# Linear attention with a following FFN on one core: k by token from the DMA queue's transpose instead of TensorE's

## The chip, the cores and the metric

One core of one Trainium2 chip runs the whole program. The metric is the device time of one execution in microseconds (us), lower is better; a kernel's time is the median of its runs.

## The reference

x has 8 batches of 1024 tokens with 512 channels. One attention layer with pre-norm and one linear FFN follow each other, both with a residual:

```python
qkv = layernorm(x) @ W_attn + b_attn            # 512 -> 3 * 512
q, k = elu(q) + 1, elu(k) + 1                   # 16 heads of 32 channels
def step(carry, inp):                           # over the tokens, in order
    kv = kv + kt[..., :, None] * vt[..., None, :]
    ksum = ksum + kt
    return (kv, ksum), (qt @ kv) / (qt @ ksum + 1e-6)
x = x + y @ W_proj + b_proj
x = x + fp16(e4m3(layernorm(x))) @ fp16(e4m3(weight)).T + bias
```

## The kernel before

The 8192 tokens are cut into 64 token tiles of 128; n numbers them. Four tiles make a block j, and 8 tiles a batch, at whose start the carried state begins anew. The main loop goes over n = 0 to 65, written out for each engine in its own order: TensorE, ScalarE (act), VectorE (dve), GpSimd (pool) and SP (sp), whose queue issues every DMA. They are tied by semaphores; each engine takes its instructions in order, so what stands behind a waiting instruction waits too.

For one block the projection makes 12 results of 128x512: i = 0 to 3 are q and 4 to 7 are k, with channels on partitions and the block's 512 tokens in the columns, and 8 to 11 are v for its four tiles, with tokens on partitions. Each is 12 matmuls of fp16 (high and low part of the data and of the weight). They are made one block ahead, three in each tile's iteration (`ahead(chunks(n))`), two before and one behind the place of `k_tokens`; in n = 59 to 61 there is one each, in n = 62 and 63 none. `phi` on ScalarE (exp and relu) and VectorE (min and add) turns q and k into features in `qk`, fp32.

For tile n TensorE goes through `scores(n)` (k against q, in halves of 64 tokens, into S), `from_state(n)` (q against the carried state), two feature results, the transposes of `k_tokens(n + 1)`, the third result, `values(n)` (masked scores times v), `update(n + 1)` (called delta here: k by token times v, which gives what the next tile adds to the state), `proj(n - 1)` and `ffn(n - 2)`. `update` needs k with tokens on partitions, as the stationary operand. That is `k_tokens`: four transposes of 128x128 fp32 on TensorE against `ident` into one bank, then one copy by ScalarE into `ktok`, which has two buffers.

ScalarE's order in iteration n is: copy of half the scores (sm), x2 to fp8 and to bf16 for tile n - 2, exp and relu of the first result, the high part of the layer norm (xnhl), exp and relu of the second, the copy of ktok for tile n + 1, exp and relu of the third, the high part of y, and the copy of ffn's result (o). VectorE and GpSimd do the norms' statistics and scaling, the low parts, the masks, the state and the residual.

Other transposes already go by the queue: the layer norm's two fp16 parts (xnhl to xt, 8 blocks of 128x128), y's two parts (yhl to yt, 8 blocks) and x2 in bf16 (x2b to x2t, 4 blocks). SP's order in iteration n is y's transpose for tile n - 1, x2's for n - 2, xt's for n + 8, a load of x for n + 10, and the store of tile n - 2, which waits for VectorE's last addition. For the last four tiles TensorE transposes y itself.

The matmul results, the transposes, delta, proj and ffn take turns in a ring of four banks of PSUM (`take`): each waits until the one four places before it has been read. In the listing S is the other half of PSUM. `raw` is a buffer of 24 KB per partition for the weights as they are loaded; its third part (raw[:, 2]) is read last by the preparation of v's weight (`s_wl` at 6).

Of the kernel before, what the change touches and what calls it, by code (L numbers as in the profile page):

```python
# [10 lines left out]
BF16 = mybir.dt.bfloat16  # L11
F8 = mybir.dt.float8e4
I32 = mybir.dt.int32

D = 512
B = 8
T = 1024
P = 128
HALF = P // 2
W = 33  # L20
NT = B * T // P
# [67 lines left out]
def build(nc, x_d, wa_d, ba_d, wp_d, bp_d, wf_d, bf_d, out_d):  # L89
    ctx = ExitStack()  # L90
    with ctx:
# [6 lines left out]
        def sem(name):  # L98
            return ctx.enter_context(nc.semaphore(f"s_{name}"))
# [51 lines left out]
        w_f = raw[:, 0, :, :]  # L151
        w_8 = raw[:, 1, 0:2, :].rearrange("p a n -> p (a n)").bitcast(F8).rearrange("p (i k n) -> p i k n", i=2, k=4)
        w_lo, w_hi = w_8[:, 0, :, :], w_8[:, 1, :, :]
        w_b = raw[:, 1, 2:4, :].rearrange("p a n -> p (a n)").bitcast(BF16).rearrange("p (k n) -> p k n", k=4)


# [4 lines left out]
        s_wft = sem("wft")  # L161
        s_xt = [sem(f"xt{t}") for t in range(4)]
        s_yt = [sem(f"yt{i}") for i in range(2)]
        s_x2t = [sem(f"x2t{i}") for i in range(2)]

        s_t1, s_qkv, s_score, s_ktr, s_delta = sem("t1"), sem("qkv"), sem("score"), sem("ktr"), sem("delta")
        s_av, s_ty, s_proj, s_ffn, s_t2, s_most = sem("av"), sem("ty"), sem("proj"), sem("ffn"), sem("t2"), sem("most")

        s_xth, s_size, s_wh, s_relu, s_whi = sem("xth"), sem("size"), sem("wh"), sem("relu"), sem("whi")
        s_xhi, s_ktok, s_scopy, s_wph = sem("xhi"), sem("ktok"), sem("scopy"), sem("wph")  # L170
        s_x28, s_x2b, s_yh, s_yth, s_o16 = sem("x28"), sem("x2b"), sem("yh"), sem("yth"), sem("o16")

        s_bn1, s_var1, s_bn2, s_var2 = sem("bn1"), sem("var1"), sem("bn2"), sem("var2")
# [24 lines left out]
        def parts(n):  # L198
            j, c = divmod(n, 4)
            return qk[j % 2], v1[j % 2], j, c  # L200
# [15 lines left out]
        def _(e):  # L216
# [66 lines left out]
                    mm = matmul(out[:, :], a, b, m == 0, m == 11)  # L283
                mm.then_inc(s_qkv, 1)

            def k_tokens(n):
                src, v, j, c = parts(n)
                cols = slice(c * P, (c + 1) * P)
                out = take(("ktok", n), s_ktok, n + 1)
                for g in range(4):  # L290
                    pe.wait_ge(s_phi, phi_count(j, 4 + g))
                transposes(out, [src[:, 4 + g, cols] for g in range(4)]).then_inc(s_ktr, 1)

            def update(n):

# [106 lines left out]
            for i in range(12):  # L402
                proj_qkv(0, i)
                if i in (0, 2, 11):
                    most((0, 2, 11).index(i) + 1)
                if i == 9:
                    k_tokens(0)
            update(0)
            for n in range(NT + 2):
                j, c = divmod(n, 4)  # L410
                if n < NT:
                    scores(n)
                    from_state(n)
                    ahead(chunks(n)[0])
                    if tail(n - 1):
                        t_y(n - 1)
                    if n + 1 < NT:
                        k_tokens(n + 1)
                    if n:
                        ahead(chunks(n)[1])  # L420
                    values(n)
                    if n + 1 < NT:
                        update(n + 1)
                    if n == 0:
                        ahead(chunks(n)[1])
                if 1 <= n <= NT:
                    proj(n - 1)
                if n == NT - 1:
                    t_y(n)
                if n >= 2:  # L430
                    t2(n - 2)
                    ffn(n - 2)

        @block.scalar
        def _(e):
# [45 lines left out]
            def ln1_parts(m):  # L481
# [2 lines left out]
                    act.wait_ge(s_xt[m % 4], 16 * (m // 4 - 1))  # L484
                copy(xnhl[:, m % 4, 0, :], xn[:, m % 2, :]).then_inc(s_xhi, 1)

            def k_tokens(n):
                act.wait_ge(s_ktr, n + 1)
                if n >= 2:
                    act.wait_ge(s_delta, n - 1)  # L490
                copy(ktok[:, n % 2, :], bank["ktok", n][:, :]).then_inc(s_ktok, 1)

            def scores(n):
                if not alone(n):
# [72 lines left out]
            phi(0, 6)  # L567
            ln1_parts(7)
            phi(0, 7)
            proj_size()  # L570
            k_tokens(0)
            ffn_half()
            for n in range(NT + 2):
                j, c = divmod(n, 4)
                if n < NT:
                    scores(n)
                    if n == 0:
                        proj_weight()
                    if n >= 2:
                        t2(n - 2)  # L580
                    ahead(chunks(n)[0][:1])
                    if n + 8 < NT:
                        ln1_parts(n + 8)
                    ahead(chunks(n)[0][1:])
                    if tail(n - 1):
                        t_y(n - 1)
                    if n + 1 < NT:
                        k_tokens(n + 1)
                    if n:
                        ahead(chunks(n)[1])  # L590
                    values(n)
                    if n == 0:
                        ahead(chunks(n)[1])
                if n == NT - 1:
                    t_y(n)
                if n >= NT:
                    t2(n - 2)
                if n >= 2:
                    ffn(n - 2)

        @block.vector
        def _(e):
# [361 lines left out]
        def _(e):  # L964
# [17 lines left out]
            def t_y(n):  # L982
                if not tail(n):
                    sp.wait_ge(s_yl, n + 1)
                    if n >= 2:
                        sp.wait_ge(s_proj, n - 1)
                    e.dma_start(yt[:, n % 2, :, :], yhl[:, n % 2, :, :].rearrange("p a n -> p (a n)"),
                                transpose=True).then_inc(s_yt[n % 2], 16)

            def t2(n):  # L990
                if n < NT - 2:
                    sp.wait_ge(s_x2b, n + 1)
# [30 lines left out]
            for t in range(4):  # L1023
                t1(4 + t)
            for n in range(NT + 2):
                if 1 <= n <= NT:
                    t_y(n - 1)
                if n >= 2:
# [38 lines left out]
```

## Time and profile before

| | |
|---|---|
| time, median of 3 runs | 1013.76 us (1013.19 to 1015.6) |
| the profiled execution | 1014.31 us, span 1012.6 us |
| TensorE busy | 982.0 us (97%) |
| VectorE, GpSimd, ScalarE busy | 69%, 53%, 46% |
| mean granted TensorE clock | 0.991 |
| DMA, mean share of 16 engines | 34.9% (the queue), 81 GB/s |
| chain that ended last | TensorE 91%, VectorE 3%, GpSimd 2% |

PE is TensorE and PEld its weight loads, DVE VectorE, ACT ScalarE, POOL GpSimd, SP SyncE, and SPq the queue's issues. Busy times are of the profiled execution and overlap between engines. L231 is the line of every matmul, L235 that of every transpose on TensorE, L439 that of ScalarE's copies, whatever their place; so the tile's name tells them apart. The granted clock is given as a share of 2.4 GHz.

### The profile page before, as it was taken

The page shows a single profiled execution, that of the slowest core. Times are in us where ns is not written, and L with a number is a line of the kernel's source. Part 1 is how long each engine was busy: PE and PEld are TensorE (multiplying, and loading weights), DVE is VectorE, ACT ScalarE, POOL GpSimd, SP SyncE. Part 2 cuts the span into 40 slices and gives each one's busy share as a digit, 9 for nine tenths or more (in the row PEclk, how much of TensorE's full clock was granted, in tenths as well). Part 3 has the DMA queues.
Part 4 walks back from the last instruction along what each step waited for, and adds up shares of the span by engine and source line. Part 5 has one row for each costly group of instructions (what it writes and reads, how often), then busy time and mean ns, then how long its engine had stood idle before and what let it go on. Part 6 is the DMA issues. An engine that isn't in the chain of part 4 may idle for free.

```text
span 1012.6 us, 43583 instructions
## 1 busy us (share of the span) xinstructions
PE 982.0 (97%) x19504; PEld 549.5 (54%) x19504; DVE 701.7 (69%) x1448; ACT 463.6 (46%) x714; POOL 535.3 (53%) x523
## 2 busy tenths in 40 slices
PE   5999999999999999999999999999999999999895
PEld 2454555555555555555555555555555555555552
DVE  6888677677767677676767767767776767754573
ACT  5753452544545364453535445254454535445222
POOL 3545675564565565465456456456456556533323
PEclk9999999999999999999999999999999999999997
DMA  8714334333334334334342244343332543322211
GB/s 271 113 35 80 94 76 81 86 77 84 80 75 91 75 75 94 72 83 88 71 96 74 71 93 79 78 88 75 83 83 75 90 77 75 81 44 54 55 35 48
DMA packets 185355, 82.51 MB, mean 81 GB/s; under 512 B 165840, under 2 KB 165840, under 8 KB 185168
## 3 DMA queue, kind: packets, MB, share of 16 engines
q1 hardware_dynamic: 185168, 79.73, 34.9%
q8 instruction: 153, 2.51, 1.0%
q14 instruction: 34, 0.28, 0.1%
HBM read 22.81 MB, written 16.78 MB: 39 GB/s over the span
## 4 chain that ended last, share of the span: by engine, by line
PE 91%; DVE 3%; POOL 2%; ACT 1%; issue 1%; DMA 0%; ACTq 0%; POOLq 0%
PE R L231 74%; PE S L231 15%; PE R L235 3%; POOL st L875 1%; DVE st L606 1%; DVE xs L696 0%; POOL xn L877 0%; POOL x L877 0%; DVE raw L800 0%; DMA xs<-in_L_attn_x 0%; POOL xs L918 0%; POOL sm L902 0%; DVE qk L629 0%; DVE wpl L778 0%; ACT qk L448 0%
## 5 line engine op out<-in xcount | busy, mean ns | idle before, releaser
L231 PE MATMUL R<-xt,wh 128*128 128x512 f16 x1024 | 306.2, 381 | 2.4 <-ACT wh L439 2.4
L629 DVE SCALAR_TENSOR_TENSOR qk<-qk,rel 128x512 f32<-128x512 f32 x128 | 141.3, 1105 | 151.1 <-ACT rel L451 151.1
L909 POOL TENSOR_TENSOR yhl<-y,yhl 128x512 f16<-128x512 f32 x60 | 69.9, 1165 | 311.2 <-ACT yhl L439 311.2
L231 PE MATMUL R<-xt,wl 128*128 128x512 f16 x512 | 194.4, 381 | 0.0
L875 POOL TENSOR_TENSOR st<-st,half 128x1 f32<-128x1 f32 x128 | 94.8, 741 | 138.3 <-DVE st L611 125.4
L231 PE MATMUL R<-wh,xt 128*128 128x512 f16 x512 | 160.3, 379 | 0.0
L231 PEld LDWEIGHTS R<-xt,wh 128*128 128x128 f16 x1024 | 96.7, 98 | 108.4 <-DVE xt L744 2.6
L231 PE MATMUL R<-wph,yt 128*128 128x512 f16 x512 | 134.6, 386 | 2.8 <-DVE yt L689 2.8
L439 ACT ACTIVATE yhl<-y 128x512 f16<-128x512 f32 x60 | 37.8, 630 | 209.5 <-DVE y L683 209.5
L448 ACT ACTIVATE qk<-R,bqk,wm 128x512 f32<-128x512 f32 x128 | 98.9, 772 | 54.0 <-PE R L231 54.0
L897 POOL TENSOR_TENSOR xs<-xs,bp 128x512 f32<-128x512 f32 x64 | 110.4, 1731 | 0.1
L623 DVE TENSOR_TENSOR xnhl<-xn,xnhl 128x512 f16<-128x512 f32 x56 | 88.3, 1576 | 22.3 <-ACT xnhl L439 22.3
L451 ACT ACTIVATE rel<-R,bqk,wm 128x512 f32<-128x512 f32 x128 | 98.5, 769 | 1.7 <-DVE qk L629 1.7
L231 PE MATMUL R<-wl,xt 128*128 128x512 f16 x256 | 97.0, 379 | 0.0
L606 DVE BATCH_NORM_STATS2 st<-xs 128x6 f32<-128x512 f32 x128 | 88.4, 690 | 5.9 <-DMA xs<-in_L_attn_x 3.7
L918 POOL TENSOR_TENSOR xs<-xs,bf 128x512 f32<-128x512 f32 x64 | 81.7, 1277 | 5.3
L231 PEld LDWEIGHTS R<-xt,wl 128*128 128x128 f16 x512 | 50.3, 98 | 61.1 <-issue 1.1
L231 PEld LDWEIGHTS S<-v,sm 64*64 64x64 f32 x4096 | 65.9, 134 | 31.1 <-issue 29.1
L231 PEld LDWEIGHTS R<-wh,xt 128*128 128x128 f16 x512 | 50.1, 98 | 55.6
L439 ACT ACTIVATE o<-R 128x512 f16<-128x512 f32 x64 | 38.3, 598 | 91.3 <-PE R L231 91.3
L231 PE MATMUL S<-v,sm 64*64 64x33 f32 x4096 | 73.2, 221 | 5.0 <-POOL sm L902 3.2
L637 DVE SCALAR_TENSOR_TENSOR v<-R,wm,bv 128x512 f32<-128x512 f32 x64 | 47.8, 747 | 42.4 <-PE R L231 42.1
(91 smaller groups left out, 1498.0 us busy)
## 6 DMA issues: line engine op xcount, KB each, us to landing
xs<-in_L_attn_x SPq DMA_DIRECT2D x64, 256.0 KB, 3.8
out<-xs SPq DMA_DIRECT2D x64, 256.0 KB, 2.4
raw<-in_L_attn_W_attn SPq DMA_DIRECT2D x3, 1024.0 KB, 9.6
xs<-in_L_attn_W_proj SPq DMA_DIRECT2D x4, 256.0 KB
raw<-in_L_ffn_weight SPq DMA_DIRECT2D x1, 1024.0 KB, 16.2
x2t<-x2b SPq DMA_TRANSPOSE x62, 2.3
xt<-xnhl SPq DMA_TRANSPOSE x60, 3.1
yt<-yhl SPq DMA_TRANSPOSE x60, 3.2
```

The costliest lines, as they stand in the source:

```text
L231: return e.matmul(out, a, b, start=start, stop=stop, skip_group_check=True)
L439: return e.activation(out, in_, ACT.Copy, **more)
L448: e.activation(dst[:, i, :], bank["qkv", j, i][:, :], ACT.Exp, scale=UN[i // 4], bias=bqk[:, i:i + 1])
L451: e.activation(rel[:, u % 2, :], bank["qkv", j, i][:, :], ACT.Relu, scale=UN[i // 4], bias=bqk[:, i:i + 1]).then_inc(s_relu, 1)
L606: e.bn_stats(row[:, 0:6], src).then_inc(s_bn, 1)
L623: e.tensor_tensor(xnhl[:, m % 4, 1, :], xn[:, m % 2, :], xnhl[:, m % 4, 0, :], ALU.subtract).then_inc(s_xlo, 1)
L629: e.scalar_tensor_tensor(qk[j % 2][:, i, :], qk[j % 2][:, i, :], 1.0, rel[:, (u - 1) % 2, :], ALU.min, ALU.add).then_inc(s_phi, 1)
L637: e.scalar_tensor_tensor(v1[j % 2][:, t, :, 0:32], heads(bank["qkv", j, 8 + t][:, :]), UN_V, heads(bv[:, :]), ALU.mult, ALU.add).then_inc( ...
L875: e.tensor_tensor(row[:, 10:11], row[:, 9:10], half[:, :], ALU.pow).then_inc(s_rs, 1)
L897: e.tensor_tensor(x, x, bp[:, :], ALU.add).then_inc(s_xb, 1)
L909: e.tensor_tensor(yhl[:, n % 2, 1, :], y[:, :], yhl[:, n % 2, 0, :], ALU.subtract).then_inc(s_yl, 1)
L918: e.tensor_tensor(x, x, bf[:, :], ALU.add).then_inc(s_x1b, 1)
```

## The change

TensorE transposes k for tile 0 only. For tile 1 and all later ones, ScalarE reads k's fp32 words (128 channels by 128 tokens, four groups) as pairs of 16-bit integers and writes them as two planes, all low halves and all high halves, into `khl` (`k_split`: two copies of 512 columns, read at a pitch of two half words). SP issues one DMA transpose of the 8 blocks into `kt` (`t_k`). ScalarE then joins the two planes into fp32 words of `ktok` (the new `k_tokens`: two copies, written at a pitch of two half words). The bits are the same as before. Both new buffers lie in raw[:, 2], two halves each, so the splits also wait for `s_wl` at 6.

`k_split(n + 2)` stands at the end of ScalarE's iteration n, behind the copy of ffn's result; `k_split(1)` stands ahead of `proj_size` before the loop. `t_k(n + 1)` stands at the head of SP's iteration n, ahead of y's transpose. The joins for n + 1 stand where the copy stood. On TensorE the four transposes and their turn in the ring of banks are gone from all iterations.

```diff
@@ -11,6 +11,7 @@
 BF16 = mybir.dt.bfloat16
 F8 = mybir.dt.float8e4
 I32 = mybir.dt.int32
+I16 = mybir.dt.int16
 
 D = 512
 B = 8
@@ -151,6 +152,9 @@
         w_f = raw[:, 0, :, :]
         w_8 = raw[:, 1, 0:2, :].rearrange("p a n -> p (a n)").bitcast(F8).rearrange("p (i k n) -> p i k n", i=2, k=4)
         w_lo, w_hi = w_8[:, 0, :, :], w_8[:, 1, :, :]
+
+        khl = raw[:, 2, 0:2, :].rearrange("p a n -> p (a n)").bitcast(I16).rearrange("p (i w n) -> p i w n", i=2, w=2)
+        kt = raw[:, 2, 2:4, :].rearrange("p a n -> p (a n)").bitcast(I16).rearrange("p (i k n) -> p i k n", i=2, k=8)
         w_b = raw[:, 1, 2:4, :].rearrange("p a n -> p (a n)").bitcast(BF16).rearrange("p (k n) -> p k n", k=4)
 
 
@@ -161,13 +165,14 @@
         s_wft = sem("wft")
         s_xt = [sem(f"xt{t}") for t in range(4)]
         s_yt = [sem(f"yt{i}") for i in range(2)]
+        s_kt = [sem(f"kt{i}") for i in range(2)]
         s_x2t = [sem(f"x2t{i}") for i in range(2)]
 
         s_t1, s_qkv, s_score, s_ktr, s_delta = sem("t1"), sem("qkv"), sem("score"), sem("ktr"), sem("delta")
         s_av, s_ty, s_proj, s_ffn, s_t2, s_most = sem("av"), sem("ty"), sem("proj"), sem("ffn"), sem("t2"), sem("most")
 
         s_xth, s_size, s_wh, s_relu, s_whi = sem("xth"), sem("size"), sem("wh"), sem("relu"), sem("whi")
-        s_xhi, s_ktok, s_scopy, s_wph = sem("xhi"), sem("ktok"), sem("scopy"), sem("wph")
+        s_xhi, s_ktok, s_khl, s_scopy, s_wph = sem("xhi"), sem("ktok"), sem("khl"), sem("scopy"), sem("wph")
         s_x28, s_x2b, s_yh, s_yth, s_o16 = sem("x28"), sem("x2b"), sem("yh"), sem("yth"), sem("o16")
 
         s_bn1, s_var1, s_bn2, s_var2 = sem("bn1"), sem("var1"), sem("bn2"), sem("var2")
@@ -283,13 +288,12 @@
                     mm = matmul(out[:, :], a, b, m == 0, m == 11)
                 mm.then_inc(s_qkv, 1)
 
-            def k_tokens(n):
-                src, v, j, c = parts(n)
-                cols = slice(c * P, (c + 1) * P)
-                out = take(("ktok", n), s_ktok, n + 1)
+            def k_tokens():
+
+                out = take("ktok", s_ktok, 1)
                 for g in range(4):
-                    pe.wait_ge(s_phi, phi_count(j, 4 + g))
-                transposes(out, [src[:, 4 + g, cols] for g in range(4)]).then_inc(s_ktr, 1)
+                    pe.wait_ge(s_phi, phi_count(0, 4 + g))
+                transposes(out, [qk[0][:, 4 + g, 0:P] for g in range(4)]).then_inc(s_ktr, 1)
 
             def update(n):
 
@@ -404,7 +408,7 @@
                 if i in (0, 2, 11):
                     most((0, 2, 11).index(i) + 1)
                 if i == 9:
-                    k_tokens(0)
+                    k_tokens()
             update(0)
             for n in range(NT + 2):
                 j, c = divmod(n, 4)
@@ -414,8 +418,6 @@
                     ahead(chunks(n)[0])
                     if tail(n - 1):
                         t_y(n - 1)
-                    if n + 1 < NT:
-                        k_tokens(n + 1)
                     if n:
                         ahead(chunks(n)[1])
                     values(n)
@@ -484,11 +486,31 @@
                     act.wait_ge(s_xt[m % 4], 16 * (m // 4 - 1))
                 copy(xnhl[:, m % 4, 0, :], xn[:, m % 2, :]).then_inc(s_xhi, 1)
 
+            def k_split(n):
+                src, v, j, c = parts(n)
+                for g in range(4):
+                    act.wait_ge(s_phi, phi_count(j, 4 + g))
+                act.wait_ge(s_wl, 6)
+                if n >= 3:
+                    act.wait_ge(s_kt[n % 2], 16 * ((n - 1) // 2))
+                words = src[:, 4:8, c * P:(c + 1) * P].bitcast(I16).rearrange("p g (t w) -> p w g t", w=2)
+                for w in range(2):
+                    made = copy(khl[:, n % 2, w, :].rearrange("p (g t) -> p g t", g=4), words[:, w, :, :])
+                made.then_inc(s_khl, 1)
+
             def k_tokens(n):
-                act.wait_ge(s_ktr, n + 1)
+                dst = ktok[:, n % 2, :]
+                if n == 0:
+                    act.wait_ge(s_ktr, 1)
+                    copy(dst, bank["ktok"][:, :]).then_inc(s_ktok, 1)
+                    return
+                act.wait_ge(s_kt[n % 2], 16 * ((n + 1) // 2))
                 if n >= 2:
                     act.wait_ge(s_delta, n - 1)
-                copy(ktok[:, n % 2, :], bank["ktok", n][:, :]).then_inc(s_ktok, 1)
+                words = dst.bitcast(I16).rearrange("p (d w) -> p w d", w=2)
+                for w in range(2):
+                    made = copy(words[:, w, :], kt[:, n % 2, 4 * w:4 * w + 4, :].rearrange("p g d -> p (g d)"))
+                made.then_inc(s_ktok, 1)
 
             def scores(n):
                 if not alone(n):
@@ -567,6 +589,7 @@
             phi(0, 6)
             ln1_parts(7)
             phi(0, 7)
+            k_split(1)
             proj_size()
             k_tokens(0)
             ffn_half()
@@ -597,6 +620,8 @@
                     t2(n - 2)
                 if n >= 2:
                     ffn(n - 2)
+                if n + 2 < NT:
+                    k_split(n + 2)
 
         @block.vector
         def _(e):
@@ -987,6 +1012,13 @@
                     e.dma_start(yt[:, n % 2, :, :], yhl[:, n % 2, :, :].rearrange("p a n -> p (a n)"),
                                 transpose=True).then_inc(s_yt[n % 2], 16)
 
+            def t_k(n):
+                sp.wait_ge(s_khl, n)
+                if n >= 3:
+                    sp.wait_ge(s_ktok, n - 1)
+                e.dma_start(kt[:, n % 2, :, :], khl[:, n % 2, :, :].rearrange("p a n -> p (a n)"),
+                            transpose=True).then_inc(s_kt[n % 2], 16)
+
             def t2(n):
                 if n < NT - 2:
                     sp.wait_ge(s_x2b, n + 1)
@@ -1023,6 +1055,8 @@
             for t in range(4):
                 t1(4 + t)
             for n in range(NT + 2):
+                if n + 1 < NT:
+                    t_k(n + 1)
                 if 1 <= n <= NT:
                     t_y(n - 1)
                 if n >= 2:
```

## Rows read from the trace of the kernel before

**Rows 1.** The page's first part: busy us, share of the span, instructions.

```profile
PE 982.0 (97%) x19504; PEld 549.5 (54%) x19504; DVE 701.7 (69%) x1448; ACT 463.6 (46%) x714; POOL 535.3 (53%) x523
```

**Rows 2.** Stretches: us; busy PE, PEld, DVE, ACT, POOL; PEclk, DMA share, GB/s.

```profile
60.00:96.00 36.00, 32.27 (x687) 18.03 (x688) 29.51 (x49) 14.32 (x23) 18.51 (x16) 0.96 0.41 72
105.00:928.00 823.00, 822.95 (x16695) 461.83 (x16694) 577.75 (x1188) 384.56 (x601) 455.48 (x436) 1.00 0.35 79
```

**Rows 3.** Chain of waits around 500 us: start us, us, what.

```profile
481.31 0.44 PE R L235 x4
...
496.40 0.44 PE R L235 x4
```

**Rows 4.** Timeline of TensorE: start us, us, what, idle before in brackets.

```profile
496.24 0.60 PE L235 MATMUL R<-ident,qk 128*128 128x128 f32 x4
...
500.43 0.76 PE L231 MATMUL R<-v,ktok 64*32 64x33 f32 x64
501.12 1.04 PE L231 MATMUL R<-wph,yt 128*128 128x512 f16 x4
```

**Rows 5.** Timeline of ScalarE, one token tile.

```profile
493.35 0.63 ACT L439 ACTIVATE x2b<-x 128x512 bf16<-128x512 fp8e4 x1
493.88 0.76 ACT L448 ACTIVATE qk<-R,bqk,wm 128x512 f32<-128x512 f32 x1
...
497.79 0.59 ACT L439 ACTIVATE ktok<-R 128x512 f32<-128x512 f32 x1
499.47 0.78 ACT L448 ACTIVATE qk<-R,bqk,wm 128x512 f32<-128x512 f32 x1 [1.09 <-PE R L231]
...
504.78 0.60 ACT L439 ACTIVATE o<-R 128x512 f16<-128x512 f32 x1 [0.78 <-PE R L231]
506.33 0.60 ACT L439 ACTIVATE sm<-S 128x512 f32<-128x512 f32 x1 [0.95 <-PE S L231]
```

**Rows 6.** Timeline of SP's queue, one middle tile and the tail.

```profile
506.49 0.34 SPq L1041 DMA_DIRECT2D out<-xs  x1
506.93 1.29 SPq L987 DMA_TRANSPOSE yt<-yhl  x1
...
957.18 0.34 SPq L1041 DMA_DIRECT2D out<-xs  x1
...
967.11 0.34 SPq L1041 DMA_DIRECT2D out<-xs  x1
...
977.46 0.34 SPq L1041 DMA_DIRECT2D out<-xs  x1
```

**Rows 7.** The tile yt: its transposes on the queue, issue to landing.

```profile
DMA to landing us min/median/max: 2.7/3.2/4.8
```

**Rows 8.** Timeline of TensorE, start and tail.

```profile
60.49 0.75 PE L231 MATMUL R<-v,ktok 64*32 64x33 f32 x64 [0.61 <-ACT ktok L439]
...
91.34 1.14 PE L231 MATMUL S<-v,sm 64*64 64x33 f32 x64 [1.58 <-POOL sm L902]
...
93.33 1.89 PE L231 MATMUL R<-wph,yt 128*128 128x512 f16 x4
...
946.51 1.14 PE L231 MATMUL S<-v,sm 64*64 64x33 f32 x64 [1.13 <-POOL sm L902]
...
961.04 0.76 PE L231 MATMUL R<-v,ktok 64*32 64x33 f32 x64
...
971.39 0.76 PE L231 MATMUL R<-v,ktok 64*32 64x33 f32 x64
...
981.16 0.46 PE L231 MATMUL R<-v,ktok 64*32 64x33 f32 x32 [0.60 <-ACT ktok L439]
```

**Rows 9.** Timeline of ScalarE, start.

```profile
74.91 0.59 ACT L439 ACTIVATE ktok<-R 128x512 f32<-128x512 f32 x1
...
91.86 0.59 ACT L439 ACTIVATE ktok<-R 128x512 f32<-128x512 f32 x1
```

**Rows 10.** Groups of TensorE's instructions by shape: busy us, mean ns, idle before.

```profile
L235 PE MATMUL R<-ident,qk 128*128 128x128 f32 x256 | 38.4, 273 | 0.0
```

## The prediction

> **What bounds the kernel now.** I read the page's first part, then the busy time by stretch, then the chain of waits, and last the timelines of each engine through one tile and through both ends of the run. TensorE is busy 982.0 of 1012.6 us [rows 1]. From 105 to 928 us it is busy for all of it, at the full granted clock (1.00, the 2.4 GHz level), while VectorE is busy 577.75, GpSimd 455.48 and ScalarE 384.56 of these 823 us [rows 2]. The reader is to see that no other engine sets the pace there. The chain of waits runs on TensorE alone, and the same piece comes back every 15.09 us (481.31, 496.40), one token tile each [rows 3]. Within that piece the four transposes of k hold 0.44 us of the chain; the last of them ends 0.60 us after the first starts, but 0.16 us of that lies under the next matmul [rows 3, 4]. Only the two ends are not set by TensorE: it waits for ScalarE's ktok at 60.49, for GpSimd's mask at 91.34 and 946.51, and for ktok again at 981.16 [rows 8].
>
> **What goes.** Of 64 groups of four transposes 63 go, those for tiles 1 to 63, which are issued in iterations n = 0 to 62. A group gives back 0.44 us only where TensorE has no wait behind it. In n = 0 to 2 there is one: delta for tile 1 waits for ktok, and values of tiles 1 and 2 wait for the mask, which hangs on VectorE's preparation of the weights; 91.34 is the last of these waits [rows 8]. In n = 59 values waits 1.13 us for the mask [rows 8]. The tiles n = 60 to 62 I count below. That leaves n = 3 to 58, 56 groups x 0.44 = 24.6 us. ScalarE's copy of ktok out of PSUM (0.59 us [rows 5]) goes as well.
>
> At this place a rule speaks another way. The Trainium skill (TensorE: Matmul & The Clock Gate, Part 4: PE-mode transpose) gives a transpose of 128x128 in 16 bits about 390 ns alone and about 275 ns in a kernel; at 4 x 275 ns a group would give back 1.1 us, an estimate from that page, and 56 groups 61.6 us in place of 24.6. The chain here shows 0.44 us for four with fp32 words [rows 3], so the trace does not agree with it as a price in a stream.
>
> **ScalarE's four copies.** Two splits and two joins take the place of one copy. None reads or writes 16-bit words at a pitch of 4 bytes in the trace of before, so the price is bounded: below by a copy of the same 512 columns from SBUF, 0.63 us, the next activation starting 0.53 us after it (493.35 and 493.88) [rows 5]; above by twice that, 1.27 us with a pitch of 1.17, if every half word cost an access of its own. I take the lower, because every copy of 512 columns there takes 0.59 to 0.63 us whichever of its types is read or written [rows 5]. A pair then takes 0.53 + 0.63 = 1.16 us.
>
> The joins start where the copy started, at 497.79, behind relu of the second feature matmul, and end at 498.95. Delta for the next tile starts at 500.43 [rows 4], 0.44 us earlier without the transposes, so at 499.99; with 0.1 us from ScalarE's end to TensorE's start the slack is 0.95 us. The cost is nothing, and without that cover all that exceeds 0.95 us would be paid per tile. Queued behind the joins is exp of the third feature matmul, which waited 1.09 us for TensorE until 499.47 [rows 5]; it moves to 499.03, and the joins let it go at about 498.9. The splits stand behind the copy of ffn's result (504.78), so they end at 504.78 + 0.53 + 1.16 = 506.47. Behind them is the copy of the scores, which waited for TensorE until 506.33 [rows 5]; it is held up by 0.1 us. It feeds the mask of values, for which TensorE never waits in the middle, being busy for all of it [rows 2], and I take the 0.1 us as covered there.
>
> **The queue.** SP now issues k's transpose ahead of y's. The store of the output goes at 506.49, 0.34 us, y's transpose at 506.93 [rows 6]; k's takes that place, since the splits are done at 506.47, and y's comes 1.3 us later. A transpose of the same 8 blocks lands 3.2 us after its issue in the median [rows 7]. In its tile k's is due when the joins must start: 499.99 - 0.1 - 1.16 = 498.7, issued at 506.93 - 15.09 = 491.84, so 6.9 us are there for 3.2; for y's the longest landing seen is 4.8 us [rows 7], still inside. Its joins follow at once. y's transpose lands some 1.3 to 2 us later than before, near 512.1, and proj wants it 15.09 us after 501.12 [rows 4], at 516.2, less 0.44. x2's transpose and x's next load move by at most that 1.3 us and have longer still. TensorE's ring of four banks loses a member, so each result now waits for another one of the tile, at the nearest proj for relu of the second feature matmul, done before the joins begin. I find no wait there.
>
> **The ends.** In n = 1 ktok (74.91 [rows 9]) stands in ScalarE's row before the third exp, on whose end y, the weights of the FFN and then the mask at 91.34 hang; the second join adds 0.53 us. In n = 2 ktok (91.86 [rows 9]) becomes 92.39, ends at 93.55, and delta, which is due behind the 1.14 us of values (91.34, now 91.87) [rows 8], comes 0.5 us late. Start: +1.0. In the tail the tiles are short. From the store to delta there are 961.04 - 957.18 = 3.86, 971.39 - 967.11 = 4.28 and 981.16 - 977.46 = 3.70 us [rows 6, 8]. The new path needs 0.44 (store) + 3.2 (landing) + 1.16 (joins) + 0.1 = 4.9 us, and the store itself comes with the tile's start. So the three tiles lose 1.0 + 0.6 + 1.2 = 2.9 us, where their removed transposes give nothing. New idle time can also take the clock down: after the wait of 1.58 us at 91.34, four matmuls of proj took 1.89 us from 93.33 on in place of 1.04 [rows 4, 8], with the granted clock at 0.96 over that stretch [rows 2]. If a drop holds for eight such matmuls it costs 2 x 0.85 = 1.7; the tail gets a wait of about 1.8 us at its last delta. Between 0 and 1.7 I take 0.9.
>
> **The sum.** -24.6 + 1.0 + 2.9 + 0.9 = -19.8 us. The profiled execution took 1014.31 us, 0.55 above the median of 1013.76 (its span is 1012.6, 1.7 us lie around it); it would come to 994.5, and the median to 994.0.
>
> **Rivals.** (1) The half words are dear. At 1.17 + 1.27 us the joins end at 500.23 and delta is 0.33 us late against 499.99 with its 0.1; that is paid in 56 tiles, 18.5 us, so 1012.5 and no change that counts. For it: no row with this pitch. Against it: types alone change nothing [rows 5]. It decides from 0.48 us more per copy. (2) k lands late: this one ends slower. If k's transpose took over 6.9 us from its issue, the joins, and behind them the third exp, would wait on ScalarE and delta on them. At 7.3 us the 0.44 is used up; at 8.0 each of 56 tiles is 1.1 - 0.44 = 0.66 us longer than before, 37 us, and with the ends' 4.9 the time is 1055. For it: three transposes now follow each other on one queue. Against it: the 3.2 us, and 4.8 at the longest [rows 7]. The Trainium skill (VectorE: DVE Perf Modes, The three transpose paths) gives 1309 ns for a 128x128 block on the DMA path against 390 ns on TensorE, and advises TensorE where the result may go to PSUM. Eight blocks in a row at that price would be 10.5 us, an estimate from that page; the trace, with 3.2 us for eight, does not agree. (3) Another loop of waits closes just below the old period, and part of the 0.44 us comes back as a wait; with half of it the time is 994.0 + 12.3 = 1006.3. The rows show no wait behind TensorE from which its distance could be read; the busiest engine after it, VectorE, works 70% of the time [rows 2], which speaks against it. (4) Each group gives back its four whole durations, 4 x 0.273 = 1.09 us [rows 10]: 0.65 more in 56 groups, 957.6 us. The chain, in which the next matmul starts 0.44 us after the first transpose [rows 3], speaks against it.
>
> **Chances.** Forecast 0.86, (1) 0.05, (2) 0.05, (3) 0.03, (4) 0.01. What this kernel's measurement can tell from no change is about 0.3%, 3 us. The forecast, (3) and (4) are faster, 0.90; (1) is the same, 0.05; (2) is slower, 0.05. The forecast's own range: without any cost at the ends 1013.76 - 24.6 = 989.2, with all 63 groups 986.0; with the ends' 4.9 twice, 998.9. The halves of (1) and (3) reach over that, so the range for 8 in 10 is 988 to 1001.
>
> **What would show it.** In the profile after: transposes with ident of qk x4 in place of x256, a steady piece of 14.65 us; splits and joins at 0.6 us each; k's transpose landing in 3 to 3.5 us; no wait of TensorE for ktok between 105 and 900 us, and three of 0.6 to 2 us in the last 50 us. Wrong would be copies of 1.1 us or more, a steady wait for ktok, or a landing over 6.9 us.

## The result and the profile after

The changed kernel takes 999.74 us in the median of four runs (999.29 to 1004.85), against 1013.48 us for the kernel before on the same chip. The ratio is 0.9873, 95% interval 0.9837 to 0.9908: 13.7 us faster, where 19.8 were forecast. The profiled executions, 999.34 and 1014.31 us, have spans of 997.4 and 1012.6 us; the readings below explain these 15.2 us, which are more than the 13.7 of the medians mostly because the profiled execution of before lies 0.8 us above its median and that of the changed kernel 0.4 below.

The page's first part after, to be read against [rows 1]:

```profile
PE 956.0 (96%) x19190; PEld 522.2 (52%) x19252; DVE 698.5 (70%) x1448; ACT 570.1 (57%) x903; POOL 534.0 (54%) x523
```

TensorE is 26 us less busy, ScalarE 106 us more. About 3 of the 26 us are not real: in 62 tiles the record of ffn's fourth matmul is missing from this trace (19190 matmuls stand beside 19252 weight loads), and its time counts as idle. In the chain of waits (start, us, what) the piece of one tile is shorter and has no transposes in it:

```profile
482.22 7.88 PE R L236 x36
...
496.88 7.88 PE R L236 x36
```

It comes back after 14.66 us where it was 15.09 [rows 3]: the 0.44 us, to the rounding. The 36 matmuls of three results now follow one another in one stretch of 7.88 us.

ScalarE through one tile, its timeline, against [rows 5]; the splits write into the buffer called raw here, since khl and kt are views of it:

```profile
481.28 1.14 ACT L441 ACTIVATE raw<-qk 128x512 int16<-128x512 int16 x2
482.34 0.60 ACT L441 ACTIVATE sm<-S 128x512 f32<-128x512 f32 x1
...
488.89 1.41 ACT L441 ACTIVATE ktok<-raw 128x512 int16<-128x512 int16 x2
490.16 0.76 ACT L450 ACTIVATE qk<-R,bqk,wm 128x512 f32<-128x512 f32 x1
```

The two copies by form over the whole run (busy us, mean ns, idle before):

```profile
L441 ACT ACTIVATE ktok<-raw 128x512 int16<-128x512 int16 x126 | 88.0, 768 | 4.3 <-DMA raw<-raw 4.3
L441 ACT ACTIVATE raw<-qk 128x512 int16<-128x512 int16 x126 | 71.8, 621 | 1.3 <-DVE qk L654 1.3
```

The splits, which read at a pitch of two half words, cost 621 ns, as a plain copy does. The joins, which write at that pitch, cost 768 ns. The pair of splits takes 1.14 us and the score copy behind it starts at once; the pair of joins ends at 490.30. TensorE's delta follows, without a wait (first line, against [rows 4]); the second line is a stall that I return to:

```profile
491.10 0.76 PE L236 MATMUL R<-v,ktok 64*32 64x33 f32 x64
...
820.79 0.59 PE L236 MATMUL R<-xt,wh 128*128 128x512 f16 x2 [1.48 <-issue]
```

The queue in the same tile, against [rows 6], and k's transpose in the page's part on DMA issues (its last number is the median time to landing):

```profile
482.50 0.34 SPq L1075 DMA_DIRECT2D out<-xs  x1
482.93 1.39 SPq L1019 DMA_TRANSPOSE raw<-raw  x1
484.42 1.25 SPq L1012 DMA_TRANSPOSE yt<-yhl  x1
```

```profile
raw<-raw SPq DMA_TRANSPOSE x63, 3.3
```

Up to here everything is as the prediction has it, but for the joins, which are dearer than it took them. The start and the tail are not. TensorE's waits in the start, against [rows 8], and stretches of the run (busy us of PE, PEld, DVE, ACT, POOL, then the granted clock, DMA share, GB/s), against [rows 2]:

```profile
60.45 0.89 PE L236 MATMUL R<-v,ktok 64*32 64x33 f32 x64 [1.84 <-ACT ktok L441]
...
77.25 0.82 PE L236 MATMUL R<-v,ktok 64*32 64x33 f32 x64 [0.92 <-ACT ktok L441]
...
94.37 0.82 PE L236 MATMUL R<-v,ktok 64*32 64x33 f32 x64 [0.84 <-ACT ktok L441]
```

```profile
57.00:62.00 5.00, 3.16 (x133) 2.13 (x132) 4.93 (x7) 2.73 (x4) 3.31 (x2) 0.85 0.02 3
77.00:84.00 7.00, 6.75 (x206) 3.83 (x207) 5.69 (x12) 3.14 (x7) 2.94 (x2) 0.76 0.27 56
94.00:98.00 4.00, 3.63 (x71) 1.75 (x72) 3.91 (x7) 0.23 (x1) 1.52 (x1) 0.57 0.56 131
105.00:928.00 823.00, 817.02 (x16844) 448.30 (x16900) 583.08 (x1209) 487.52 (x783) 464.35 (x445) 1.00 0.46 99
```

The wait for ktok at 60.45 is 1.84 us where it was 0.61, and the clock is at 0.85 around it; behind the wait at 77.25, which is new, it is 0.76, and behind the one at 94.37 it is 0.57, nearly the 1.2 GHz level. The first two drops are new (1.00 in the same stretches before); the third is not, since the kernel before has 0.68 from 94 to 98 us, behind its wait for the mask. The tail on TensorE's timeline:

```profile
939.23 0.75 PE L236 MATMUL R<-v,ktok 64*32 64x33 f32 x64 [1.86 <-ACT ktok L441]
940.94 1.74 PE L236 MATMUL R<-wph,yt 128*128 128x512 f16 x4 [0.97 <-DMA yt<-yhl]
942.48 1.91 PE L236 MATMUL R<-wpl,yt 128*128 128x512 f16 x4
...
953.36 0.75 PE L236 MATMUL R<-v,ktok 64*32 64x33 f32 x64 [1.45 <-ACT ktok L441]
...
964.64 0.46 PE L236 MATMUL R<-v,ktok 64*32 64x33 f32 x32 [2.88 <-ACT ktok L441]
965.03 1.89 PE L236 MATMUL R<-wph,yt 128*128 128x512 f16 x4
966.71 1.87 PE L236 MATMUL R<-wpl,yt 128*128 128x512 f16 x4
```

and the chain of waits through its first part:

```profile
933.72 0.34 SPq L1075
...
934.15 2.03 SPq L1019
...
936.28 4.53 DMA yt<-yhl
...
940.94 4.45 PE R L236 x12
...
948.42 3.39 DMA raw<-raw
```

Four waits, and behind two of them proj's matmuls at the lower clock: 1.74, 1.91, 1.89 and 1.87 us for four where 1.04 is the full clock's time [rows 4]. The granted clock is 0.66 from 940 to 945 and from 965 to 970 us. Behind the wait of 1.45 us it stays at 1.00: not every wait takes it down.

To put the difference in its place I cut each span at the start of delta for tile 4 and for tile 59, both read from TensorE's timeline:

| us | before | after | difference | forecast |
|---|---|---|---|---|
| start, to delta of tile 4 | 109.32 | 110.50 | +1.2 | +0.6 |
| middle, 55 tiles | 827.15 | 806.06 | -21.1 | -24.2 |
| tail, from delta of tile 59 | 76.13 | 80.84 | +4.7 | +3.8 |
| span | 1012.6 | 997.4 | -15.2 | -19.8 |

The forecast of the start is its 1.0 less one group of 0.44 that falls before this cut. The measured +1.2 is too small: the first delta began at 51.02 us in the profile of before and at 50.20 in this one (between 49.80 and 51.02 in all profiles). Counted from there, delta of tile 4 comes after 58.30 us before and 60.30 us after, so the start lost 2.0 us.

### The profile page after: what moved, and what is told of

It is laid out like the page before. It is cut to its first block, busy times and chain, and to the rows that moved or that the text cites. A ratio compares the mean times of both kernels' runs of the same rounds, so it can differ in the third digit from the quotient of the medians.

```text
span 997.4 us, 43420 instructions
## 1 busy us (share of the span) xinstructions
PE 956.0 (96%) x19190; PEld 522.2 (52%) x19252; DVE 698.5 (70%) x1448; ACT 570.1 (57%) x903; POOL 534.0 (54%) x523
## 4 chain that ended last, share of the span: by engine, by line
PE 90%; DVE 3%; ACT 2%; POOL 2%; issue 2%; DMA 1%; SPq 0%; POOLq 0%; ACTq 0%
PE R L236 75%; PE S L236 14%; DVE st L631 1%; DMA raw<-raw 1%; DVE xs L721 1%; POOL st L900 1%; ACT ktok L441 1%; DMA yt<-yhl 0%; POOL xn L902 0%; DVE raw L825 0%; POOL x L902 0%; ACT qk L450 0%; PE R L240 0%; ACT rel L453 0%; DMA xs<-in_L_attn_x 0%
## 5 line engine op out<-in xcount | busy, mean ns | idle before, releaser
L236 PE MATMUL R<-wh,xt 128*128 128x512 f16 x512 | 158.0, 379 | 0.0
L441 ACT ACTIVATE ktok<-raw 128x512 int16<-128x512 int16 x126 | 88.0, 768 | 4.3 <-DMA raw<-raw 4.3
L721 DVE SCALAR_TENSOR_TENSOR xs<-R,wm,xs 128x512 f32<-128x512 f32 x64 | 48.0, 750 | 41.8 <-PE R L236 41.8
```

The lines of the kernel that those rows point to most:

```text
L236: return e.matmul(out, a, b, start=start, stop=stop, skip_group_check=True)
L441: return e.activation(out, in_, ACT.Copy, **more)
L721: e.scalar_tensor_tensor(x, bank["proj", n][:, :], UN_P, x, ALU.mult, ALU.add).then_inc(s_x1, 1)
```

## The experiments

My account was: TensorE gives back 0.44 us a tile in the middle and nothing else changes there; what is missing is lost at both ends, where the way of k through ScalarE and the queue is longer than the time there is. The rival was that the new path costs a little in every tile. The runs were made on four chips (e1 to e4, e5 to e8, e9 to e11, e12), each time beside the kernel before, whose median was 1013.72 to 1014.42 us; the ratios are to it, and across chips they compare better than the times. The cuts of the table above are repeated for each run at the end of this section.

**e1, the changed kernel again.**

> The changed kernel once more, as the reference for the next three. Both theories expect a ratio of 0.985 to 0.989 to the kernel before, some 999.5 us. My account of the result: the middle gives back 0.44 us a tile (21.7 us over tiles 4 to 59), the start loses 1.8 and the tail 4.7 us. The rival account: the queue and ScalarE hold up the middle a little everywhere, and the ends are as before.

1001.50 us (998.84 to 1003.08), ratio 0.9878, 0.9855 to 0.9902. Start 110.15, middle 806.33, tail 83.72. So the start and the middle repeat within 0.4 us and the tail does not: it is 2.9 us longer than in the first profile, with waits for ktok of 1.34, 1.70 and 3.15 us and proj's matmuls at the lower clock behind all three. Between these two profiles the spread is in the tail.

**e2, the last three tiles' k through TensorE.**

```diff
+K_PE = (0, 61, 62, 63)
...
-            def k_tokens():
+            def k_tokens(n):
+                if n not in K_PE:
+                    return
...
                     if tail(n - 1):
                         t_y(n - 1)
+                    if n + 1 < NT:
+                        k_tokens(n + 1)
```

k_split and t_k return for tiles in K_PE, and the counts that are waited for are adapted.

> k of tiles 61, 62 and 63 goes through TensorE again, all else as changed. If the tail's loss is the way store, transpose on the queue, joins, which is longer than a short tile, it gives back 3 to 5 us: 995 to 996.5, and no wait for ktok over 1 us in the last 60 us. If the tail's loss is only the clock or chance stalls, nothing or less than 1 us: 999 to 1000.

993.28 us (991.10 to 994.00), ratio 0.9799, 0.9782 to 0.9815: 8.2 us below e1 and 6.5 below the first measurement, more than the 3 to 5 I expected. TensorE's timeline in the tail:

```profile
938.87 0.76 PE L244 MATMUL R<-v,ktok 64*32 64x33 f32 x64
...
949.22 0.76 PE L244 MATMUL R<-v,ktok 64*32 64x33 f32 x64
...
958.99 0.57 PE L244 MATMUL R<-v,ktok 64*32 64x33 f32 x32 [1.33 <-ACT ktok L454]
959.49 1.04 PE L244 MATMUL R<-wph,yt 128*128 128x512 f16 x4
```

The waits at delta of tiles 61 and 62 are gone, the one at 63 is 1.33 us, above the 1 us that I allowed, and proj behind these three stays at 1.04. The tail of the span is 74.71 us. So the new path costs the tail some 6 to 9 us, not the 4.7 of the table, because the kernel before has a stall in its own tail, with matmuls at the lower clock behind it:

```profile
950.09 0.36 PE L231 MATMUL R<-v,ktok 64*32 64x33 f32 x13 [1.87 <-issue]
950.38 1.89 PE L231 MATMUL R<-wph,yt 128*128 128x512 f16 x4
```

In the changed kernel a stall of this kind lies in the middle (820.79). A slow clock in the tail is not the new path's alone either: e2 has matmuls of 1.89 and 1.65 us from 928.15 on, behind a wait of 1.55 us for the mask. A difference of two traces hides a cost where something unrelated has moved away from the same place.

**e3, tiles 1 to 3 through TensorE.** The same edit with `K_PE = (0, 1, 2, 3)`.

> k of tiles 1, 2 and 3 goes through TensorE again. If the start's loss comes from the second join (and its 0.77 us) in ScalarE's row, delta of tile 3 is back at about 92.6 us and the time falls by 1.5 to 2 us, to about 997.8. If the split of tile 2 or the new transposes on the queue delay the preparation of the weights, less than 0.7 us.

998.27 us (996.48 to 999.65), ratio 0.9850, 0.9834 to 0.9867: 3.2 us below e1, where I expected 1.5 to 2. Delta of tile 1 and the stretch around it:

```profile
59.70 0.75 PE L244 MATMUL R<-v,ktok 64*32 64x33 f32 x64 [0.61 <-ACT ktok L454]
```

```profile
57.00:62.00 5.00, 4.38 (x143) 3.06 (x142) 4.93 (x7) 1.94 (x3) 3.34 (x2) 1.00 0.01 3
```

The wait is the 0.61 us of before and the clock there stays at 1.00. Delta of tile 4 comes at 107.84, 2.3 to 2.7 us earlier than with the joins; counted from the first delta it is 57.61 us against 60.30 and, in e1, 60.35, so 2.7. The middle is also 1.2 to 1.5 us shorter, because the stall of 1.48 us is not there in this kernel; that part is no merit of the start. The cause of the start's loss is shown: k's way through ScalarE for tiles 1 to 3. How much of it is the joins' own time and how much the clock behind the longer wait, e6 shows below.

**e4, both ends through TensorE.** `K_PE = (0, 1, 2, 3, 61, 62, 63)`.

> Both ends through TensorE, the middle through the queue. By my account the sum of the two, 5 to 6.5 us less than the changed kernel: 993 to 994.5, ratio 0.980 to 0.981. By the rival account within 1 us of the changed kernel.

989.38 us (988.01 to 990.99), ratio 0.9764, 0.9747 to 0.9781: 12.1 us below e1, and the sum of e2 and e3 is 11.4 (above the 5 to 6.5 expected, as both parts were). The two ends add up; the stall is absent here too, which makes 1.5 us of it. This kernel beats both.

**e5, no k by token after tile 0.** Delta of every tile is made from tile 0's ktok; splits, transposes and joins are left out.

```diff
-                pe.wait_ge(s_ktok, n + 1)
+                pe.wait_ge(s_ktok, 1)
...
-            k_split(1)
...
-                    if n + 1 < NT:
-                        k_tokens(n + 1)
...
-                if n + 1 < NT:
-                    t_k(n + 1)
```

> No k by token after tile 0 at all: no transposes on TensorE, no splits, queue transposes or joins; delta of every tile is made from tile 0's ktok, which is all that is left out. If the removed transposes are worth 0.44 us each and all else was given back at the ends: tile period 14.66 us as in the changed kernel, and a time of 987 to 989.5, near the version with both ends on TensorE (989.4). If the new path also costs in the middle, the period is below 14.6 and the time below 985. If four whole durations were to be had, 957.

990.72 us (990.38 to 990.92), ratio 0.9776, 0.9760 to 0.9792, 1.2 us above my range. The period is 14.66, the middle 805.21 us, against 806.06 with the whole new path in it. Of the difference of 0.85 us, 0.82 lies in the one tile with the stall (15.67 against 16.49 us). So 252 activations and 63 transposes on the queue cost the middle nothing that shows, which refutes the rival; and leaving them out gains nothing over e4, which has them.

**e6, TensorE's transposes put back as dead work.** Nobody reads their result; the joins wait for them, as the copy did.

```diff
+            def k_dead(n):
+                src, v, j, c = parts(n)
+                cols = slice(c * P, (c + 1) * P)
+                out = take(("dead", n), s_ktok, n + 1)
...
+                transposes(out, [src[:, 4 + g, cols] for g in range(4)]).then_inc(s_dead, 1)
```

> The changed kernel, and TensorE transposes k as before as well; the result in PSUM is read by nobody. If the gain is TensorE's 0.44 us alone, the period is back at 15.10 and the time is 0.44 x 56 = 24.6 us over the changed kernel, 1024 to 1026, slower than the kernel before by the ends' cost. If the new path has slack that this restores, the tail is a little cheaper: 1022.

1018.57 us (1017.37 to 1021.78), ratio 1.0057, 1.0036 to 1.0078. The chain of waits:

```profile
481.13 0.44 PE R L241 x4
...
496.22 0.44 PE R L241 x4
```

The piece is back at 15.09 us with 0.44 in it, and the middle is 827.05 us, that of before to 0.1. So all of the middle's gain is TensorE's time. The total is 17 us over e1 and not the 24.6 expected over the changed kernel: the start is 1.0 to 1.4 us and the tail 1.4 to 4.3 us shorter than with the transposes gone, and the middle has no stall. With the new path and without its gain the kernel is slower than before, by 4.9 us in the medians: that is what the ends cost while TensorE still has its transposes.

This run also separates the joins from the clock in the start. The joins stand in ScalarE's row as in the changed kernel, but with the transposes ahead of it TensorE's wait is shorter, and the clock stays up:

```profile
60.52 0.75 PE L237 MATMUL R<-v,ktok 64*32 64x33 f32 x64 [1.41 <-ACT ktok L452]
```

```profile
77.00:84.00 7.00, 6.82 (x153) 3.70 (x152) 6.75 (x13) 2.33 (x5) 1.61 (x2) 1.00 0.12 21
```

It is 1.00 from 57 to 62 and from 62 to 66 us as well, where the changed kernel has 0.85 and 0.77. Delta of tile 1 begins 10.26 us after the first delta in e6 and 10.25 in the changed kernel; from there to delta of tile 2 e6 takes 15.39 us, the changed kernel 16.80, e3 15.16. So some 1.4 of the 2.7 us are the clock.

**e7 and e8, one and two more copies ahead of the joins** of every tile from 4 on, to measure the slack in place of arguing it. The edit is e8's; e7 has `range(1)`.

```diff
+                if n >= 4:
+                    act.wait_ge(s_wfd, 7)
+                    for i in range(2):
+                        copy(pad[:, i, :], kt[:, n % 2, 0:4, :].rearrange("p g d -> p (g d)"))
                 words = dst.bitcast(I16).rearrange("p (d w) -> p w d", w=2)
```

> The changed kernel with one more copy of 512 half words on ScalarE ahead of the joins of every tile from 4 on, 0.53 us. The joins end 0.66 us before delta must have them in the trace after (490.30 with 0.14 to go, delta at 491.10), so 0.53 fits: the period stays 14.66 and only the tail grows, by up to 1.6 us: 1000 to 1003. If the joins are already at the edge, 0.53 x 56 = 30 us more.

1004.83 us (1003.97 to 1006.30), ratio 0.9918, 0.9903 to 0.9933. The period stays at 14.66 and the middle is 806.59 us: the first copy is hidden whole. The tail grows to 86.99 us, which takes the time above the 1000 to 1003 that I allowed.

> Two more copies ahead of the joins from tile 4 on, 1.06 us against a slack of 0.66: delta late by 0.4 us in the three tiles of four in which the joins follow a feature's relu, 42 x 0.4 = 17 us, and up to 3 us in the tail: 1017 to 1022, slower than the kernel before. If the slack is larger than I read it: under 1005.

1024.44 us (1022.43 to 1026.78), ratio 1.0111, 1.0088 to 1.0134, above the 1017 to 1022 expected. Delta in a middle tile on TensorE's timeline, and ScalarE's copies and joins:

```profile
500.32 0.75 PE L237 MATMUL R<-v,ktok 64*32 64x33 f32 x64 [0.45 <-ACT ktok L442]
```

```profile
482.57 1.14 ACT L442 ACTIVATE raw<-raw 128x512 int16<-128x512 int16 x2
483.61 1.40 ACT L442 ACTIVATE ktok<-raw 128x512 int16<-128x512 int16 x2
```

In two or three tiles of each block of four the period is 15.17, 0.51 us more for a second copy of 0.53; the middle grows by 19.5 us. So the edge lies between one and two copies, as read from the trace: the joins end at 490.30, 0.14 us pass to TensorE's start, and 0.66 us are left to delta at 491.10. Delta waits 0.45 us in e8, so that the slack comes out at 1.06 - 0.45 = 0.61 us. The two added copies read the same tile as the joins and write without a pitch: two take 1.14 us and two joins 1.40 us, start to end, so it is the write at a pitch of two half words that costs the joins their extra time.

**e9, the split earlier.** It goes ahead of y's high part, where ScalarE idles, and k's transpose ahead of the store, which waits for VectorE.

```diff
+                    if n + 2 < NT:
+                        k_split(n + 2)
                     values(n)
...
-                if n + 2 < NT:
-                    k_split(n + 2)
...
                     load_x(n + 10)
+                if 2 <= n and n + 2 < NT:
+                    t_k(n + 2)
```

> The changed kernel with the split of tile n + 2 ahead of the copy of y's high part instead of behind ffn's, where ScalarE idles 2.46 us, and k's transpose behind the load of x, ahead of the store and its wait. Issue moves some 4 us earlier in the middle and 2.5 to 3 us in the tail. If the tail's loss is the way behind the store, it shrinks by most of its 4.7 us without any transpose on TensorE, and the middle stays at 14.66: 994 to 996. If the joins themselves, or the queue's bandwidth, cause it, 999 to 1001.

996.76 us (995.47 to 998.65), ratio 0.9828, 0.9810 to 0.9847: 4.7 us below e1, 5.1 by the ratios. The queue in a middle tile:

```profile
493.83 1.24 SPq L1019 DMA_TRANSPOSE raw<-raw  x1
498.35 0.34 SPq L1078 DMA_DIRECT2D out<-xs  x1
```

k's transpose is issued 4.5 us ahead of the store instead of 0.43 us behind it. The middle (806.05 us) doesn't notice; the tail is 77.05 us, against 80.84 and 83.72. So the greater part of the tail's loss is the way behind the store. What is left over e2's 74.71 are waits for ktok of 0.34, 1.00 and 2.12 us in which k has landed already and ScalarE goes through the joins.

**e10, k's transpose third on the queue.** Three lines of SP's row change places: y's, x2's, then k's.

> The changed kernel with k's transpose behind y's and x2's in SP's row, issued about 2.7 us later. The trace after leaves 6.6 us from issue to the joins' latest start in the middle, and 2.7 + 3.3 = 6.0 of it would be used: the period stays 14.66. In the tail there is no slack, so each of three tiles loses some 2 us more, less the 1 us by which y came late: 1003 to 1007. If a landing after three transposes takes over 4 us, the middle pays as well: over 1010.

1025.59 us (1022.13 to 1027.36), ratio 1.0107, 1.0082 to 1.0133: a miss of mine by 20 us. SP's queue in a middle tile:

```profile
485.61 0.34 SPq L1075 DMA_DIRECT2D out<-xs  x1
486.05 1.29 SPq L1012 DMA_TRANSPOSE yt<-yhl  x1
488.21 1.20 SPq L1027 DMA_TRANSPOSE x2t<-x2b  x1
489.50 1.26 SPq L1019 DMA_TRANSPOSE raw<-raw  x1
```

k's transpose goes 3.9 us behind the store, not 2.7 behind its old place: I had added the issues before it, but x2's transpose waits for ScalarE's x2b. That uses up the slack: most tiles keep 14.66, some pay, one of them 1.52 us, 6.9 us in the middle in all (812.98). In the tail TensorE waits 4.70, 5.45, 4.26 and 5.83 us for ktok, and the tail is 99.84 us. This is the prediction's rival 2 made true by an edit: k issued some 3.5 us later (it lands as fast, 2.7 us in the median) makes the kernel slower than before. Against the changed kernel that is 16 to 19 us in the tail and 6.9 in the middle, where rival 2 had nearly all of it in the middle.

**e11 and e12, the early split with ends through TensorE**: e9 with tiles 1 to 3, and with tiles 1 to 3 and 61 to 63.

> e9 with tiles 1 to 3 through TensorE. The start's gain of e3 (3.2 us, with the clock staying up at 60 us) and the tail's of e9 should add up: 990.5 to 993. If it is not below e4 (989.4), the tail's tiles are better off on TensorE.

991.69 us (989.83 to 993.72), ratio 0.9778, 0.9753 to 0.9802: 5.1 us below e9, on the same chip. It is not below e4 (0.9764), and its tail is 77.42 us against 74.85: the last tiles are better off on TensorE.

> e4 (tiles 1 to 3 and 61 to 63 through TensorE) with the early split of e9 for the rest. If only the ends lost, nothing is left for the early split to give in the middle: 988.5 to 990, the same as e4 (989.4) within its 1.5 us, period 14.66. If the split behind ffn's copy holds something up in the middle, below 988.

990.89 us (988.90 to 991.46), ratio 0.9760, 0.9743 to 0.9778. The same as e4 by the ratio. With the ends on TensorE the place of the split is worth nothing.

The spans cut as above, us:

| | start | middle | tail | span |
|---|---|---|---|---|
| before | 109.32 | 827.15 | 76.13 | 1012.6 |
| changed | 110.50 | 806.06 | 80.84 | 997.4 |
| e1 changed, again | 110.15 | 806.33 | 83.72 | 1000.2 |
| e2 tail on TensorE | 110.59 | 805.70 | 74.71 | 991.0 |
| e3 start on TensorE | 107.84 | 804.82 | 84.94 | 997.6 |
| e4 both | 108.21 | 804.74 | 74.85 | 987.8 |
| e5 no k by token | 108.63 | 805.21 | 74.86 | 988.7 |
| e6 dead transposes | 109.13 | 827.05 | 79.42 | 1015.6 |
| e7 one more copy | 109.82 | 806.59 | 86.99 | 1003.4 |
| e8 two more copies | 110.23 | 825.59 | 88.48 | 1024.3 |
| e9 early split | 111.80 | 806.05 | 77.05 | 994.9 |
| e10 k third | 111.88 | 812.98 | 99.84 | 1024.7 |
| e11 early, start | 107.03 | 805.15 | 77.42 | 989.6 |
| e12 early, both | 108.74 | 805.31 | 74.45 | 988.5 |

## Why the prediction was right, and where its terms were off

The mechanism was right, and the time lies within 988 to 1001, but near its upper end: 999.74 us, and e1, the same kernel again, came to 1001.50, just outside. The forecast of 994.0 was 5.7 us too low, and the measured gain is 13.7 of 19.8 us. By the prediction's steps:

- **What goes, 56 x 0.44 = 24.6 us.** The price of a group is right (15.09 to 14.66 in the trace; back to 15.09 in e6), and rival 4, with whole durations, is refuted: the period did not fall by 1.09 us. The middle gained 21.1 of 24.2 us. 1.8 of the missing 3.1 is one tile of 16.49 us, most of it the stall at 820.79, for which the trace names no releaser; the kernel before has its own in the tail. The rest, 1.3 us, is spread over tiles of 14.7 to 14.9 us and over the second tile of each block, which shrank by 0.32 to 0.44 us. It is there in e4 (no stall, 804.74 us) and in e5 (no new path) too, so it is neither. What holds these tiles is not settled.
- **ScalarE's copies.** The splits are 621 ns (0.63 forecast). The joins are 768 ns, between the two bounds and nearer the lower: the pair takes 1.41 us against 1.16, 0.25 of the possible 1.3 us extra. They hide as said, with 0.66 us of slack in place of 0.95, most of the difference being these 0.25 us; e7 and e8 bracket it.
- **The queue.** k lands 3.3 us after its issue in the median (3.2 forecast), and 6.6 us are there for it in the middle. Rival 2 had no ground there. But the sentence that y's transpose has room was true only of the middle: in the tail it was issued 2.1 us behind k's, landed after 4.53 us and held proj up by 0.97 us.
- **The start, 1.0 us.** Counted from the first delta it was 2.0 at tile 4 where 0.6 was forecast, and e3 gives back 2.7. I left out n = 0: I named the wait for ktok there and gave the second join no price, and it grew from 0.61 to 1.84 us and took the clock down with it. The clock, which I priced in the tail alone, is about half of the loss (e6).
- **The tail, 2.9 + 0.9 us.** This is the step that was mis-sized. Against e2 the new path costs 6.1 us there in the first profile and 9.0 in e1. Two of its terms were too small and one was missing. The way from the store to delta took 5.51, 5.37 and 5.23 us (stores at 933.72, 947.99 and 959.41) where 4.9 was forecast: against the 3.86, 4.28 and 3.70 of before that is 4.3 us and not 2.9. The joins and the step from their end to TensorE's start make 0.27 us of the excess each time (1.39 + 0.14 us), landings of 3.3 to 3.6 us the rest. The clock was to cost 0.9 us and costs 0.70 + 0.87 + 0.85 + 0.83 = 3.3 us in the sixteen matmuls above, of which before and e2 have 1.5 too, elsewhere in their tails. y's wait of 0.97 us was not in the sum. The mechanism was right: e9 shortens just this way and takes most of the loss back.
- **Rivals 1 and 3** did not come: no wait for ktok and no other loop in the middle. e5 shows that without k's new path the middle is not shorter. Of the signs named, joins at 0.6 us and three waits of 0.6 to 2 us in the tail were missed, with 0.77 and with 1.86, 1.45 and 2.88.

## What to carry to other kernels

Work taken from the engine that runs through is worth its spacing in the chain (here 0.44 us for four transposes), not its recorded duration (1.09), and the engine that takes it over may be given up to the slack of its next consumer; that slack can be read from the trace and tested with one or two dummy copies. A longer way that hides in the middle of a pipeline shows at its ends, where the stages are short: put the old way there and the new one in the middle (e4), or start the new one as early as its data allow (e9). Price a wait of TensorE with the clock behind it.

## What the runs showed of the hardware

- ScalarE writes 512 half words at a pitch of two in 768 ns and without a pitch in about 610 (two in 1.14 us, overlapped); reading at that pitch costs nothing (621 ns). The Trainium skill (ScalarE: Activation LUTs, What ACT_TABLE_LOAD costs) gives 186 ns + 0.833 ns a column for an activation with immediate operands, fp32 and bf16 alike. For 512 columns that is 612 ns, an estimate from that page. The splits and the added copies agree with it; the joins are 25% over it, and here the measurement decides.
- In the start and the tail of the changed kernel waits of 0.84 to 2.88 us stood near stretches with TensorE's granted clock at 0.57 to 0.85, though not all of them (1.00 behind 1.45 us), and the eight matmuls from 940.94 on and the eight from 965.03 on took 1.7 to 1.9 times their time at full clock. The tail differs between profiles with k's last tiles behind the store on the queue (80.84, 83.72 and, in e3, 84.94 us) and hardly between those without (74.45 to 74.86 in e2, e4, e5 and e12).
- TensorE has a stall without a releaser whose place goes with its own program and not with the time. In the changed kernel, e1, e2 and e7 to e10, whose TensorE programs are the same up to there, 1.20 to 1.48 us stand before the same matmul, behind the 15,948th weight load, at 820.5 to 837.5 us. In the kernel before and in e6, with the same 64 groups of transposes on TensorE, 1.87 us stand behind the 18,404th, near 950. e5 has 0.62 us at 818.89. In e3, e4, e11 and e12, which have twelve transposes more at the start, no such gap in the middle is over 0.3 us. It is worth 1.2 to 1.9 us of a comparison in which a few instructions of TensorE are added or removed. What it waits for was not tried.
